# A graph network's two edge passes: softmax sums turned back one tile further behind, source indices held in SBUF, and the setup's search started first

## The reference

```python
# layer 0, softmax aggregation
m = relu(feat[src]) + EPS
seg_max = segment_max(m, dst, N)
ex = exp(m - seg_max[dst])
a = ex / segment_sum(ex, dst, N)[dst]
msg = segment_sum(a * m, dst, N)
return (feat + msg) @ W + b
# layer 1, message network; _mlp is a product, a relu and a normalisation over all rows
edge_feat = _mlp(edge_attr, W_edge, ...)
message = _mlp(concatenate([x[row], x[col], edge_feat], axis=1), W_msg, ...)
return segment_sum(message, col, N) + node_feat
```

## Time and profile before

| | |
|---|---|
| median of 3 runs | 5516.88 us (5506.9 to 5519.22) |
| the profiled execution | 5542.31 us, span 5540.4 us |
| granted TensorE clock, mean | 0.819 |
| PE busy | 3184.8 us |
| DVE busy | 2663.9 us |
| POOL busy | 2500.9 us |
| ACT busy | 1558.5 us |
| mean memory traffic | 145 GB/s |

### The profile page before, as it was taken

The page is one execution under the profiler, slowest core; times in us unless marked ns, Lnnn a source line. Parts: engine busy times, 40 slices in busy tenths (PEclk is TensorE's granted clock), DMA queues, the critical chain, the costliest instruction groups (busy, mean ns, idle before and its releaser), DMA issues.

```text
span 5540.4 us, 71225 instructions
## 1 busy us (share of the span) xinstructions
PE 3184.8 (57%) x18737; PEld 2336.6 (42%) x18737; DVE 2663.9 (48%) x5882; ACT 1558.5 (28%) x3677; POOL 2500.9 (45%) x2580
## 2 busy tenths in 40 slices
PE   0444444444465555455545555320117999999999
PEld 0333333333443333333333333210006777778777
DVE  3777777777644444454445554540001144433333
ACT  1666666676222222222222222210000011111000
POOL 6555555555555555555555555677770000000000
PEclk9999999999966666666666666655558999999999
DMA  6555555555223333333333333210005756666776
GB/s 198 173 179 178 172 181 174 175 181 169 66 79 102 102 97 101 98 101 100 100 95 102 102 101 102 73 56 0 0 12 202 269 195 248 247 250 248 256 277 230
DMA packets 418286, 801.74 MB, mean 145 GB/s; under 512 B 237496, under 2 KB 294684, under 8 KB 391980
## 3 DMA queue, kind: packets, MB, share of 16 engines
q1 hardware_dynamic: 270182, 591.99, 31.8%
q0 software_dynamic: 82320, 90.28, 7.8%
q10 hardware_dynamic: 65718, 118.62, 5.7%
HBM read 581.84 MB, written 218.74 MB: 144 GB/s over the span
## 4 chain that ended last, share of the span: by engine, by line
PE 28%; issue 23%; another core or an unknown queue 22%; DVE 12%; ACT 7%; SPq 3%; ACTq 2%; POOL 1%; DMA 1%; DVEq 1%; POOLq 0%
PE ps L1166 16%; PE ps L1096 6%; DVE second L1675 3%; SPq L629 2%; DVE area L1691 2%; ACT ps L1215 2%; DVE second L1685 2%; ACT dump L1219 1%; ACT out_ring L1231 1%; ACT relu_dump L1215 1%; ACT out_ring L1239 1%; ACTq L1241 1%; PE ps L921 1%; PE ps L928 1%
## 5 line engine op out<-in xcount | busy, mean ns | idle before, releaser
L939 PE MATMUL ps<-ident,area 96*128 96x96 f32 x2352 | 435.6, 352 | 1083.8 <-ACT out_ring L1231 416.3
L779 POOL DMA_INDIRECT area<-src_table,idx_src x784 | 751.0, 958 | 510.2 <-DMA idx_src<-src_dram 261.0
L779 POOL DMA_INDIRECT area<-relu_table,idx_src x784 | 740.4, 944 | 533.4 <-issue 324.8
L939 PEld LDWEIGHTS ps<-ident,area 96*128 96x128 f32 x2352 | 347.0, 210 | 1208.1 <-issue 855.6
L1662 DVE TENSOR_TENSOR_SCAN area<-flags,area,ps 96x512 f32<-96x512 int8 x196 | 249.7, 1274 | 960.5 <-ACT dump L1219 743.0
L1166 PE MATMUL ps<-second,area 128*128 128x288 bf16 x5194 | 650.7, 286 | 0.2 <-DVE second L1809 0.2
L1166 PEld LDWEIGHTS ps<-second,area 128*128 128x128 f16 x5194 | 508.3, 98 | 127.6 <-DVE second L1809 0.5
L1627 DVE SCALAR_TENSOR_TENSOR second<-second,area,ps 128x512 bf16<-128x512 f32 x784 | 538.5, 743 | 0.0
L788 POOL DMA_INDIRECT adj<-copies_ring,cell_ring x392 | 389.0, 992 | 326.2 <-DVE cell_ring L1643 206.4
L921 PE MATMUL ps<-second,w_ef_scaled 96*96 96x512 f32 x392 | 313.2, 893 | 288.2 <-ACT second L1263 173.9
L1096 PE MATMUL ps<-early,area 128*128 128x288 bf16 x2401 | 328.5, 293 | 259.6 <-issue 259.6
(11 more groups left out here) (330 smaller groups left out, 4657.5 us busy)
## 6 DMA issues: line engine op xcount, KB each, us to landing
area<-adj SPq DMA_DIRECT2D x147, 1632.0 KB
area<-adj SPq DMA_DIRECT2D x55, 1568.0 KB
adj<-early SPq DMA_DIRECT2D x102, 816.0 KB
soft_sums<-out_ring ACTq DMA_DIRECT2D x196, 384.0 KB
second<-key_dram SPq DMA_DIRECT2D x98, 512.0 KB
area<-dst_table SPq DMA_DIRECT2D x784, 48.0 KB
sums<-out_ring ACTq DMA_DIRECT2D x196, 192.0 KB
second<-caps_dram SPq DMA_DIRECT2D x98, 192.0 KB
```

Source lines behind the costliest of these rows:

```text
L779: pool.indirect_dma_start(out=src_rows[:, s, c, :], out_offset=None, in_=gather_table[p], in_offset=bass.IndirectOffsetOnAxis(ap=idx_src[s ...
L939: last = nc.tensor.transpose(ps[:, b, c * F:(c + 1) * F], r[:, (s * CH + c) * P:(s * CH + c + 1) * P], ident[0:F, 0:F])
```

## The change

1. The softmax pass turns back and copies back two tiles behind instead of one, on PE and on ACT.
2. In the setup DVE finds the chunks before the two subtractions of the attribute parts.
3. All source indices are loaded once into SBUF (`src_cols`, 392 KB) during the setup; POOL reads a chunk's column there. The load of idx_src for each pair of tiles and its waits are gone, and the later load of src_cols for the node stage too.
4. POOL's two edge passes are written out in a straight line; the increments of dmas_begun are gone. The order of gathers and scatters stays.
5. attr_parts holds 12 rows, each stored once; the load of attributes reads them three times over into its 36 rows. w_edge_parts is stored in three pieces.

```diff
-        idx_src = [sb(f"idx_src{h}", [P, 2 * CH], i32) for h in range(RING // 2)]
...
+        shared = KB * PARTS_F // 2 - CN
+        src_cols = early[:, shared:].bitcast(i32)
...
+        def two_before(step, u, s):
+
+            if s >= 2:
+                step(u, s - 2)
+            elif not isinstance(u, int) or u:
+                step(u - 1, RING + s - 2)
...
+            sp.dma_start(src_cols, src_cols_in).then_inc(idx_landed, 16)
...
             for i in range(PARTS):
                 sp.wait_ge(attr_cast, i + 1)
-                for j in range(PARTS):
-                    at = (i * PARTS + j) * EDGE_DIM
-                    sp.dma_start(attr_parts[at:at + EDGE_DIM, :].rearrange("a e -> (a e)").rearrange("(p j) -> p j", p=P),
-                                 attr_bf[i]).then_inc(soft_stored, 16)
+                sp.dma_start(attr_parts[i * EDGE_DIM:(i + 1) * EDGE_DIM, :].rearrange("a e -> (a e)").rearrange("(p j) -> p j", p=P),
+                             attr_bf[i]).then_inc(soft_stored, 16)
...
-                    wait(sp, src_gathered[s], use * 16 * CH)
-                    wait(sp, src_gathered[s + 1], use * 16 * CH)
-                    sp.dma_start(idx_src[h][:, :], src_in[one, :, :].rearrange("a p c -> (a p) c")).then_inc(idx_landed[h], 16)
-
                     wait(sp, e["hid"], t + 2 - RING)
                     sp.dma_start(attr[:, s:s + 2, :].rearrange("p s e -> p (s e)"),
-                                 attr_parts[:, bass.ds(t * TE, 2 * TE)]).then_inc(attr_landed[h], 16)
+                                 attr_parts[:, bass.ds(t * TE, 2 * TE)].unsqueeze(0).to_broadcast([PARTS, PARTS * EDGE_DIM, 2 * TE]))\
+                      .then_inc(attr_landed[h], 16)
...
-                    over_tiles(pool, gather)
+                    pool.wait_ge(idx_landed, 16)
+                    for t in range(ET):
+                        gather(t)
                 else:
                     pool.wait_ge(adj_cleared, 16 * 2 * JOBS)
-                    over_tiles(pool, gather, scatter_of_two_before)
-                    for s in (RING - 2, RING - 1):
-                        scatter(EI - 1, s)
+                    for t in range(ET + 2):
+                        if t < ET:
+                            gather(t)
+                        if t >= 3:
+                            scatter(t - 3)
+                    scatter(ET - 1)
...
-                    over_tiles(pe, turn_and_project, lambda u, s: tile_before(turn_back, u, s))
-                    turn_back(EI - 1, RING - 1)
+                    over_tiles(pe, turn_and_project, lambda u, s: two_before(turn_back, u, s))
+                    for s in (RING - 2, RING - 1):
+                        turn_back(EI - 1, s)
...
-                    over_tiles(act, soften, lambda u, s: tile_before(copy_back, u, s))
-                    copy_back(EI - 1, RING - 1)
+                    over_tiles(act, soften, lambda u, s: two_before(copy_back, u, s))
+                    for s in (RING - 2, RING - 1):
+                        copy_back(EI - 1, s)
```

More of the change, by code:

```diff
@@ L137, in build @@
         rank_dram = dram("rank_dram", [EP], i8)
-        attr_parts = dram("attr_parts", [AK, EP], bf16)
+        attr_parts = dram("attr_parts", [PARTS * EDGE_DIM, EP], bf16)
         key_dram = dram("key_dram", [EP])
@@ L239, in build @@
         w_part = [sb(f"w_part{i}", [AK, F], bf16) for i in range(PARTS)]
-        setup = parts_of(early)
+        shared = KB * PARTS_F // 2 - CN
+        src_cols = early[:, shared:].bitcast(i32)
+        setup = parts_of(early[:, 0:shared])
         zeros = setup(P, KB * P // 4).bitcast(f16)
@@ L363, in build @@
         diags_made, rows_spread = sem("diags_made"), sem("rows_spread")
-        idx_landed, flags_landed, attr_landed, ranks_landed = [
+        idx_landed = sem("idx_landed")
+        flags_landed, attr_landed, ranks_landed = [
             [sem(f"{name}{h}") for h in range(RING // 2)]
-            for name in ("idx_landed", "flags_landed", "attr_landed", "ranks_landed")]
+            for name in ("flags_landed", "attr_landed", "ranks_landed")]
         src_gathered = ring_sems("src_gathered")
@@ L555, in _ @@
                 sp.wait_ge(attr_cast, i + 1)
-                for j in range(PARTS):
-                    at = (i * PARTS + j) * EDGE_DIM
-                    sp.dma_start(attr_parts[at:at + EDGE_DIM, :].rearrange("a e -> (a e)").rearrange("(p j) -> p j", p=P),
-                                 attr_bf[i]).then_inc(soft_stored, 16)
+                sp.dma_start(attr_parts[i * EDGE_DIM:(i + 1) * EDGE_DIM, :].rearrange("a e -> (a e)").rearrange("(p j) -> p j", p=P),
+                             attr_bf[i]).then_inc(soft_stored, 16)
             sp.wait_ge(w_split, 1)
[L561 to L564, removed]
+            for j in range(PARTS):
+                rows = slice(j * PARTS * EDGE_DIM, (j + 1) * PARTS * EDGE_DIM)
+                sp.dma_start(w_edge_parts[rows, :], w_part[j][rows, :]).then_inc(soft_stored, 16)
             sp.wait_ge(consts_made, 2)
@@ L769, in _, with gather, scatter @@
                 wait_for_tables(pool, p)
-                def gather(u, s):
-                    use, t = p * EI + u, u * RING + s
-                    wait(pool, idx_landed[s // 2], (use + 1) * 16)
+                def gather(t):
+                    s = t % RING
                     wait(pool, e["turned"], t - RING + 1)
-                    pool.sem_inc(dmas_begun, 1)
-                    for c in range(CH):
-                        pool.indirect_dma_start(out=src_rows[:, s, c, :], out_offset=None, in_=gather_table[p],
-                                                in_offset=bass.IndirectOffsetOnAxis(ap=idx_src[s // 2][:, s % 2 * CH + c:s % 2 * CH + c + 1], axis=0))\
+                    for c in range(t * CH, (t + 1) * CH):
+                        pool.indirect_dma_start(out=src_rows[:, s, c % CH, :], out_offset=None, in_=gather_table[p],
+                                                in_offset=bass.IndirectOffsetOnAxis(ap=src_cols[:, c:c + 1], axis=0))\
                             .then_inc(src_gathered[s], 16)
-                def scatter(u, s):
-                    wait(pool, redirected, u * RING + s + 1)
-                    pool.sem_inc(dmas_begun, 1)
+                def scatter(t):
+                    s = t % RING
+                    pool.wait_ge(redirected, t + 1)
                     for c in range(NOW):
@@ L1453, in _ @@
             v.tensor_copy(chunk_i, chunk_f).then_inc(chunk_found, 1)
+            dve.wait_ge(attr_cast, 1)
+            v.tensor_tensor(attr_rest, attr_f, attr_bf[0], ALU.subtract).then_inc(attr_left, 1)
             dve.wait_ge(x_landed, 32)
             v.tensor_scalar(h_sb, x_sb[:, :, :], 0.0, MSG_EPS, ALU.max, ALU.add).then_inc(relu_made, 1)
+            dve.wait_ge(attr_cast, 2)
+            dve.wait_ge(attr_left, 1)
+            v.tensor_tensor(attr_rest, attr_rest, attr_bf[1], ALU.subtract).then_inc(attr_left, 1)
             dve.wait_ge(seq_landed, 32)
@@ L1553, in cells_of_edges @@
                 chain.do(v.tensor_scalar(key[:, :], src_cols, P - 1, None, ALU.bitwise_and))
-                chain.do(v.tensor_scalar(src_cols, src_cols, 7, None, ALU.logical_shift_right))
+                chain.do(v.tensor_scalar(src_block, src_cols, 7, None, ALU.logical_shift_right))
                 chain.do(v.scalar_tensor_tensor(w1, node_cols, float(P), key[:, :], ALU.mult, ALU.add))
-                chain.do(v.scalar_tensor_tensor(node_cols, w1, float(KB), src_cols, ALU.mult, ALU.add))
+                chain.do(v.scalar_tensor_tensor(node_cols, w1, float(KB), src_block, ALU.mult, ALU.add))
                 chain.do(v.scalar_tensor_tensor(cell[:, :], node_cols, 7, low, ALU.logical_shift_left, ALU.bitwise_or))
```

26 lines of the change are left out of this document (6 added, 20 removed).

## The result

The changed kernel takes 5344.42 us (median of 4 runs, 5332.68 to 5347.41) against 5516.61 for the kernel before: ratio 0.9694, 95% interval 0.9678 to 0.9711. It is 172 us faster; 66 were forecast. The time lies in the stated range, near that of rival 1 (5323), though not by its mechanism, so that nearness is luck.

A forecast was written before the change was run, and what follows sets the result against it. No engine was full; waits decided, with PE's completions late while POOL issues unbroken. Setup −20, softmax −31, message −15, sum −66: 5476 us profiled, 5451 as median; range 5300 to 5600.

The forecast's parts named there:

- rival 1: Both edge passes: cycles grow by a tile, to three in softmax and four in message; −194, 5323 us; chance 0.18.
- The setup: Before the softmax pass: POOL's searches start at 12 instead of 33.89 us; −20 taken, bounds −22 and 0.
- The lag: Softmax pass, PE and ACT turning and copying back two tiles behind: 0 taken, at most −47 us.
- Completions held by POOL's unbroken issuing: Edge passes: PE's completions reach other engines late while POOL issues without a pause, and come free when it stops.
- The sign for DVE's unnamed wait: Softmax pass: DVE's "remote" wait stays about 244.6 us; below 150 or above 350 would each speak for a rival.
- rival 2: Both edge passes: POOL's pauses for idx_src were pure waste; −20−103−256 = −379, 5138 us; chance 0.08.
- Behind it lies a pause of some 3.1 us: Softmax pass, after POOL's run of two or three tiles: 6.55 or 6.03 us a tile against 6.50; weighed, −31.
- POOL loses the loop's registers and an increment a tile, hidden, as POOL waits for others anyway: POOL's edge passes in a straight line: the saved work is hidden behind waits, so no gain was counted.
- The message pass: A redirect pause of 8.3 us stays after three or four tiles: +53 or −82 us, halfway −15.
- rival 3: Slower: POOL without idx_src pauses holds others up oftener, message redirect pause 8.3 us or longer; +43, 5560 us; chance 0.20.
- The baseline: Cycle times the forecast compared with: 6.50 us a tile in the softmax pass, 10.15 in the message pass.
- Rival 4: Message pass: attribute loads come late, +105 us on top of the forecast, 5556 us; chance 0.04.

The follow-up runs named there:

- A rest a tile: Changed kernel with POOL clearing 1152 columns that nothing reads, and waiting for that, behind each softmax tile's four gathers: 5379.5 us, ratio 0.9764.
- half the issues: Changed kernel with two of each softmax tile's four gathers replaced by plain loads that SP issues, same bytes: 5238.3 us, ratio 0.9508.
- 179 or 268 GB/s: Changed kernel with softmax gathers from tile 4 fetching half the bytes: 5346 us; or with a second 816 KB clear a pair there: 5346.4 us.

## Why the prediction was off

- **The setup**: −20 forecast, −18 measured, at the place named (search at 11.87 for "near 12").
- **The lag**: 0 forecast, 0 measured from both sides. That PE's wait for the copy would fall (410.5 to 221.0) and bring nothing held too.
- **Completions held by POOL's unbroken issuing**: right in the softmax pass. A rest a tile removes the unnamed waits, half the issues remove them, and 179 or 268 GB/s in place of 196 don't. In the message pass it is not shown: with the rests ACT's unnamed waits stay (655.5 us against 663.7).
- **The sign for DVE's unnamed wait** was badly chosen. Below 150 us it was to speak for rival 2, and it fell to 96.9 though rival 2's time is far off: shorter pauses lower this wait too.
- **"Behind it lies a pause of some 3.1 us"** is the step that failed in the softmax pass. The two-tile cycle that I gave 0.6 came in most cycles, but with 11.65 us, not 13.1: the pause is 1.95. I took 3.1 from a kernel in which the pauses stood behind twelve gathers or held a wait for the indices. It has two parts, and both shrank: from POOL's last DMA to the first unnamed start of DVE or ACT 2.26 us before and 1.74 now, from there to POOL's next gather 0.74 and 0.23 (medians). And I added the pause to full tiles of 5.0, whose last 0.3 us is already pause. −128 instead of −31.
- **"POOL loses the loop's registers and an increment a tile, hidden, as POOL waits for others anyway"** failed in both passes: a cost that I put at nothing. The straight line was worth 35 and 51 us. In the message pass POOL comes back 0.7 us sooner after the others' release, in some 75 pauses, an estimate of 50 us from these medians; in the softmax pass the reason stays open.
- **The message pass**: −61 instead of −15. The index pauses did turn into others, as I had it: taking them away brought 10 of the 61. The pauses for the redirect were not 8.3 but 6.8 us behind three tiles, where rival 3 wanted 8.3 or more, and 3.2 behind two.
- **The baseline** had an error that went the other way. I compared the new cycles with one slow cycle of each pass (6.50 and 10.15 a tile) and not with the pass as a whole (6.41 and 9.93). With those the same sum gives −13 and +28 instead of −31 and −15, and −5 in all. That the forecast was no further off is luck.
- **Rival 1** came near in time by cycles of three and four tiles; what came were cycles of two in the softmax pass and of two or three in the message pass, with shorter pauses.
- **Rival 2** would have had all 359 us of index pauses; 103 came off in sum. The rule of the Trainium skill (SBUF — State Buffer, "Who interferes with whom"), that PE and ACT wait on nobody, is one on ports. It does not describe what ACT sees here: in the softmax pass its unnamed waits, 106 us before two of its steps, shrink to 2 with a rest of POOL a tile. Whether a port has any part in it no run shows.
- **Rival 4**, the late attribute load: the waits are there (54.0 us against 7.7), and without a price.

What the runs leave open is how the rest works in the message pass, why 0.92 us of it brings nothing there and 1.35 do, and through which part of the chip the completions go.

## What to carry to other kernels

When several engines wait "remote" for work that ended long ago, look at what POOL was issuing: compare the end of the matmul with the start of its reader, and both with the end of POOL's run. A pause that looks like a loss can be what lets the others proceed, so price its removal as "what will POOL do now, and who is held meanwhile", and try a rest on purpose; here a clear of 1.1 us a tile was worth 162 us in one pass and cost 35 in the other, where POOL is the bound once nothing is held. And check afterwards that the waits which it was to remove are gone: in the message pass they were not. Work at the end of a wait, such as a loop's, can lie on the path even if the engine is idle half of the time.

## What was unexpected of the hardware

- POOL resting 1.35 us behind every six indirect DMAs: message pass 1885 to 1734 us. 0.92 us: nothing. 0.45 us: nothing. ACT's unnamed waits there stay.
- POOL's pauses in the softmax pass by the length of the run before them: 1.8 us behind four gathers and behind eight, 2.5 behind twelve.
- In the softmax pass 156 of the 179 unnamed waits of DVE and ACT end in POOL's pauses; with half the issues none is left.
- The same load of attributes, read three times over from 12 rows and not once from 36, had PE wait 54.0 us in place of 7.7.
